# Windowed attention on one core: where ScalarE squares the queries, and where VectorE inverts the row sums

## The chip, the cores and the metric

One core of a Trainium2 chip runs the whole program in one launch. The metric is the device time in microseconds (us), as the median of several executions. PE is TensorE, ACT is ScalarE, DVE is VectorE, POOL is GpSimd.

## The reference

The input x is (4, 512, 256). A gated linear recurrence, a cross attention block with its own MLP, and then two layers of windowed attention with an MLP follow each other. Only the attention of the two layers is touched. Its core, for each of the two layers:

```python
q, k, v = jnp.split(shift_token(x) @ wqkv, 3, axis=-1)      # 8 heads of 64
q = l2norm(q) * qs;  k = l2norm(k) * ksc
q, k = rotary_xpos(q, k)                 # q*cos*scale + rotate_half(q)*sin*scale, k likewise
sim = einsum('bhwid,bhwjd->bhwij', q * 8, [previous window, own window] of k)
attn = softmax(where(mask, -max, sim));  out = einsum(attn, v)
x = x + out @ wo
```

The windows are 128 tokens. Each of the four sequences has four of them, so a layer has 16. The first window of a sequence has no predecessor and sees 128 keys, the others see 256.

## The kernel before, in words

The five engines run hand written instruction streams, joined by semaphores. Each wait is written out (`wait_ge(semaphore, count)`), and each engine executes its stream strictly in the order of the code. There is no planner.

The attention of a layer is a software pipeline over 16 windows n, with w the window's place in its sequence (0 to 3). In step n every engine's `window` function does the work on four tiles at once: scores, softmax and output of window n, transposition of the keys and queries of n+1 (`one`), projection of q, k and v, rotation and norms of n+2 (`two`), and the transposed input of n+3 (`three`). `two` holds in 14 of the 16 steps of a layer: the last two have nothing left to project. The eight heads are handled in four pairs i = 0 to 3; the pairs 0 and 1 use one couple of PSUM banks for scores, the pairs 2 and 3 another. A pair is two heads, so "the exponentials of a pair" are two instructions.

PE (`window`, L1944): scores of n (`score_pairs`, L1895); probabilities by values of n-1 (`weigh_values`, L1919); the projections of q and k of n+2 into banks 0 and 1 (`qkv` with i = 0 and 1, six matmuls each, recorded at L1593); transposition of the keys of n+1 (L1874); transposition of the probabilities of the pairs 0, 1, 2 (`transpose_probs`, L1905); transposition of the queries of n+1 (L1882), which waits for ACT's copy of the keys out of the same bank 2; the pair 3 of L1905; transposition of the spread reciprocal row sums (`transpose_sums`, L1929), which waits for POOL; the projection of v (L1593 again); the transposition of x of n+3 (L1851); the output projection of n-1 (L1941). `transpose_probs` waits until all four exponentials of its half (pairs 0 and 1, or 2 and 3) are done: the pairs 2 and 3 both wait for all eight.

ACT (`window`, L1482): `exps` for the pairs 0 to 3 (L1460, two instructions a pair, each with an accumulator read that gives the row sum), the square of the queries of n+2 (`square(n + 2, 0)`, L1431, which waits for their projection), the copy of the transposed keys of n+1 (`keys`, L1441), the square of the keys (L1431), the copies of the transposed probabilities (L1472), of the queries (L1447), of the sums (L1480), of v (L1436) and of x (L1423).

DVE (`window`, L1071): the masking with the row minimum for the eight heads (`masked`, L1048), `normalise` of n-1 (L1063), the norm scaling of the keys of n+1 (`norm_keys`, L1039), the reciprocal of the row sums (`invert_sums`, L1055, after all eight exponentials), the three rotation products of the queries of n+2 (`rope_products(..., 0)`, L1019 and twice L1024, after their square), those of the keys (`rope_products(..., 1)`), the sum of squares (L1031), the residual (L1069), the low part of x (L1101).

POOL: spreads the reciprocals over the head columns (L558), adds the rotation products of the queries and then of the keys (L551), computes the inverse norms (L567, L569), scales the queries (L573), splits MLP weights (L582, L584) and copies x (L543). It spreads before it rotates.

The waits that matter for the order:

```python
def square(n, i):   act.wait_ge(c_p, 3 * n + i + 1)      # projection i of tile n is done
def exps(n, w, i):  act.wait_ge(c_tt, 8 * n + 4 * (i // 2) + 4)
def transpose_probs(n, w, i): pe.wait_ge(c_ex, 8 * n + 4 * (i // 2) + 4)
def transpose_q(n, par):      pe.wait_ge(c_kt, n + 1)    # keys copied out of bank 2
def transpose_sums(n):        pe.wait_ge(c_rb, n + 1)    # POOL has spread the reciprocals
```

Of the kernel before, what the change touches and what calls it, by code (L numbers as in the profile page):

```python
# [27 lines left out]
TT = T // P  # L28
# [47 lines left out]
def build(nc, x, ctx_in, cols_in, rows_in, w_in, w_gate, w_out, wq, wk, wv, wo_x, pos_bias,  # L76
          w1_x, w2_x, lcols_in, qk_scale, rope, wqkv, wo_l, wm_l, out):
    with ExitStack() as ctx:
# [596 lines left out]
        def _(dve):  # L675
# [336 lines left out]
            def rope_products(n, w, i):  # L1012

                src = bank[i][:, :].rearrange("p (h d) -> p h d", d=DH)
                dve.wait_ge(c_sq, 2 * n + i + 1)
                if not (isinstance(n, int) and n == 0):
                    dve.wait_ge(c_add, 2 * n - 1 + i)
                cos = rope_l[:, 2 * i, w:w + 1, :].to_broadcast([P, HEADS, DH])
                dve.tensor_tensor(rot[:, 2 * i, :].rearrange("p (h d) -> p h d", d=DH), src, cos, ALU.mult)\  # L1019
                    .then_inc(c_rope, 1)  # L1020
                rotated = rot[:, 2 * i + 1, :].rearrange("p (h d) -> p h d", d=DH)
                for lo, other in ((0, DH // 2), (DH // 2, 0)):
                    sin = rope_l[:, 2 * i + 1, w:w + 1, lo:lo + DH // 2].to_broadcast([P, HEADS, DH // 2])
                    dve.tensor_tensor(rotated[:, :, lo:lo + DH // 2], src[:, :, other:other + DH // 2], sin,  # L1024
                                      ALU.mult).then_inc(c_rope, 1)

            def sum_squares(n):

                dve.wait_ge(c_sq, 2 * n + 2)
                dve.wait_ge(c_clip, n)  # L1030
                dve.tensor_reduce(norms[:, 0, :], squares[:, :, :].rearrange("p i (h d) -> p (i h) d", d=DH), AX_X,  # L1031
                                  ALU.add).then_inc(c_ss, 1)

            def norm_keys(n, par):

                dve.wait_ge(c_add, 2 * n + 2)
                dve.wait_ge(c_rn, n + 1)
                k = k_tok[:, par, :].rearrange("p (h d) -> p h d", d=DH)
                dve.tensor_tensor(k, k, norms[:, 2, HEADS:2 * HEADS].unsqueeze(2).to_broadcast([P, HEADS, DH]),  # L1039
                                  ALU.mult).then_inc(c_kn, 1)  # L1040

            def masked(n, w, i, first=False):

                nk = 2 * P if w else P
                wait_alone(dve, c_qk, 2 * n + i // 2 + 1)
                for e in range(2):
                    logits = bank[SCORES[i // 2] + e][:, (i % 2) * 2 * P:(i % 2) * 2 * P + nk]
                    dve.tensor_tensor_reduce(logits, logits, mask[:, 2 * P - nk:2 * P], 1.0, FAR, ALU.add, ALU.min,  # L1048
                                             row_min[:, w % 2, 2 * i + e:2 * i + e + 1]).then_inc(c_tt, 1)

            def invert_sums(n, w):

                dve.wait_ge(c_ex, 8 * n + 8)
                dve.wait_ge(c_rb, n)
                dve.reciprocal(row_rsum[:, :], row_sum[:, w % 2, :]).then_inc(c_ri, 1)  # L1055

            def normalise(n):

                dve.wait_ge(c_rt_out, n + 1)
                dve.wait_ge(c_pv, n + 1)  # L1060
                if not (isinstance(n, int) and n == 0):
                    dve.wait_ge(c_wo, n)
                dve.tensor_tensor(o_t[:, :, :].rearrange("p c t -> p (c t)"), bank[3][:, :], rsum_t[:, :], ALU.mult)\  # L1063
                    .then_inc(c_ot_out, 1)

            def att_residual(n, tile):

                dve.wait_ge(c_wo, n + 1)
                dve.tensor_tensor(inner[:, tile, :], inner[:, tile, :], bank[2][:, 0:D], ALU.add).then_inc(c_res, 1)  # L1069

            def window(n, t, w, l, prev, one, two, three):  # L1071
                for i in range(KI):
                    masked(n, w, i)
                if prev:
                    normalise(n - 1)
                if one:
                    norm_keys(n + 1, (w + 1) % 2)
                invert_sums(n, w)
                if two:
                    rope_products(n + 2, (w + 2) % TT, 0)  # L1080
                    rope_products(n + 2, (w + 2) % TT, 1)
                    sum_squares(n + 2)
                elif w == 2:
                    mlp_aggr(l * NB)
                if prev:
                    att_residual(n - 1, t - 1)
                if three:
                    x_low(n + 3, (w + 3) % TT, bank[1][:, 0:D])
                elif w == 1:
                    for i in range(TT):  # L1090
                        mlp_stats(l * NB, 0, i, 0)
                elif w == 2:
                    mlp_norm(l * NB, 0, 0)
                else:
                    input_low(l * NB)

            def x_low(n, w, src):

                dve.wait_ge(c_xt_out, n + 1)
                columns = slice(w * P, (w + 1) * P)  # L1100
                dve.tensor_tensor(x_lo[:, :].rearrange("p (c t) -> p c t", t=T + 1)[:, :, columns],  # L1101
                                  src.rearrange("p (c t) -> p c t", t=P),
                                  x_hi[:, :].bitcast(F32).rearrange("p (c t) -> p c t", t=T + 1)[:, :, columns],
                                  ALU.subtract).then_inc(c_xt_lo, 1)

            def mlp_stats(m, b, t, par):

                dve.wait_ge(landed[par], 32 * (m // 2) + 32)
                for i, src in enumerate((inner[:, b * TT + t, 0:P], shifts[par][:, t, :])):
                    dve.bn_stats(stats[:, t, 6 * i:6 * i + 6], src).then_inc(d_stats, 1)  # L1110

            def mlp_aggr(m):
                for t in range(TT):
                    wait_alone(dve, d_stats, 8 * m + 2 * t + 2)
                    dve.bn_aggr(mean_var[:, t, :], stats[:, t, :]).then_inc(d_aggr, 1)

            def mlp_norm(m, b, par):

                dve.wait_ge(d_rstd, m + 1)
                dve.wait_ge(d_tp, 2 * m)  # L1120
                for t in range(TT):
                    for i, src in enumerate((inner[:, b * TT + t, 0:P], shifts[par][:, t, :])):
                        dve.tensor_scalar(normed[:, t, i * P:(i + 1) * P], src, mean_var[:, t, 0:1],
                                          rstd[:, t:t + 1], ALU.subtract, ALU.mult).then_inc(d_norm, 1)

            def input_low(m):

                for c in range(KD):
                    dve.wait_ge(d_in_hi, 2 * m + c + 1)
                    dve.tensor_tensor(t_lo[:, c, :], h_t[:, c, :], t_hi[:, c, :].bitcast(F32), ALU.subtract)\  # L1130
                        .then_inc(d_in_lo, 1)
# [122 lines left out]
        def _(act):  # L1254
# [99 lines left out]
            def exps(b):  # L1354

                for m in range(KD):
                    act.wait_ge(b_kbias, 2 * b + m + 1)
                    act.activation(ek[:, m, :], bank[2 + m][:, :], ACT.Exp, bias=kstat[:, m, 2:3]).then_inc(b_ek, 1)
                    if m:
                        exp_q(b, 0)  # L1360
# [66 lines left out]
            def square(n, i):  # L1427

                act.wait_ge(c_p, 3 * n + i + 1)
                act.wait_ge(c_ss, n)  # L1430
                act.activation(squares[:, i, :], bank[i][:, :], ACT.Square).then_inc(c_sq, 1)  # L1431
# [50 lines left out]
            def window(n, w, l, prev, one, two, three):  # L1482
                exps(n, w, 0)
                exps(n, w, 1)
                exps(n, w, 2)
                exps(n, w, 3)
                if two:
                    square(n + 2, 0)
                if one:
                    keys(n + 1, (w + 1) % TT)  # L1490
                if two:
                    square(n + 2, 1)
                if not one:
                    mlp_scaled(l * NB, l)
                for i in range(KI - 1):
                    probs_transposed(n, w, i)
                if one:
                    queries(n + 1)
                probs_transposed(n, w, KI - 1)
                sums_transposed(n)  # L1500
                if two:
                    values(n + 2, (w + 2) % TT)
                if three:
                    x_transposed(n + 3, (w + 3) % TT, bank[1][:, 0:D])
                if not one:
                    mlp_rounded(l * NB)
# [665 lines left out]
```

## Time and profile before

| what | value |
|---|---|
| median of 3 executions | 992.8 us (991.03, 992.8, 993.05) |
| span of the profiled execution, first to last instruction | 990.8 us |
| PE busy | 924.9 us, 93% of the span |
| DVE busy | 675.9 us, 68% |
| ACT busy | 513.9 us, 52% |
| POOL busy | 422.6 us, 43% |
| granted TensorE clock, mean | 0.981 |

No separate time of the profiled execution is listed, only its span; the median lies 2.0 us above that span and the fastest execution 0.2 us above it. The attention steps of the first layer run from about 367 to 573 us of the span, those of the second from about 686 to 887 us. A step is read from the start of its first score matmul (L1895) to the next step's. The timeline gives for each engine the start, the duration, the line and the count of instructions merged, and in brackets the idle time ahead and what ended it.

### The profile page before, as it was taken

To read this page: it belongs to the slowest core of one execution; us is meant where nothing else is said; L and a number is where in the kernel's file an instruction comes from. 1 tells how busy PE (TensorE), PEld (TensorE's weight loads), DVE (VectorE), ACT (ScalarE), POOL (GpSimd) and SP (SyncE) were. 2 spreads that over 40 slices of the span, in tenths; PEclk is the share of its full clock that TensorE was granted. 3 is DMA by queue.
4 is the path that set the end of the run, shared out by engine and by line. 5 is a ranking of instruction groups with operands and counts; after the bars stand their busy time and mean duration, and the time that the engine had idled before them with its cause. 6 is when DMAs were issued, how large, how long until landed. Compare 5 with 4: busy or idle time off the path is not lost.

```text
span 990.8 us, 17519 instructions
## 1 busy us (share of the span) xinstructions
PE 924.9 (93%) x5688; PEld 774.2 (78%) x5688; DVE 675.9 (68%) x1706; ACT 513.9 (52%) x1221; POOL 422.6 (43%) x420
## 2 busy tenths in 40 slices
PE   5889996999999988999999899999999999889998
PEld 4668875787878866888888678887888888778887
DVE  6878797558687677677767555567766667735563
ACT  5467751313131426767666644454766666654443
POOL 5333354112221357767676400006776767631110
PEclk9889998999999999999999999999999999999999
DMA  7200123000000000000001030000000000000001
GB/s 261 70 1 16 48 65 112 1 1 0 0 0 1 1 23 1 2 23 0 22 0 33 12 105 15 4 25 2 2 24 0 22 0 12 27 15 17 31 25 46
DMA packets 15716, 26.34 MB, mean 27 GB/s; under 512 B 1642, under 2 KB 12256, under 8 KB 14896
## 3 DMA queue, kind: packets, MB, share of 16 engines
q1 hardware_dynamic: 15664, 25.69, 8.0%
q8 instruction: 27, 0.44, 0.2%
q14 instruction: 25, 0.20, 0.1%
HBM read 20.53 MB, written 2.10 MB: 23 GB/s over the span
## 4 chain that ended last, share of the span: by engine, by line
PE 72%; DVE 11%; ACT 6%; issue 3%; POOL 3%; SPq 3%; DMA 2%; ACTq 0%; DVEq 0%; POOLq 0%
PE bank L1593 33%; PE bank L1941 5%; PE bank L1895 5%; PE bank L1919 5%; PE bank L1801 5%; PE bank L1905 4%; ACT probs L1460 3%; PE bank L1764 2%; PE bank L1882 2%; PE bank L1747 1%; SPq L352 1%; DVE y L820 1%; PE bank L1929 1%; PE bank L2014 1%; PE bank L2011 1%
## 5 line engine op out<-in xcount | busy, mean ns | idle before, releaser
L1460 ACT ACTIVATE probs<-bank,row_min 128x256 f32<-128x256 f32 (+1 forms) x256 | 110.4, 458 | 120.1 <-DVE row_min L1048 120.1
L569 POOL TENSOR_TENSOR norms<-norms,minus_half 128x16 f32<-128x16 f32 x32 | 93.6, 2924 | 2.7
L1048 DVE CUSTOM_DVE_ANT_0 bank<-bank,mask 128x256 f32<-128x256 f32 (+1 forms) x256 | 90.7, 425 | 5.9 <-PE bank L1895 5.7
L1593 PE MATMUL bank<-wqkv_hi,x_hi 128*128 128x512 f32 x192 | 82.4, 429 | 1.8 <-DVE rot L1024 1.1
L1593 PE MATMUL bank<-wqkv_lo,x_hi 128*128 128x512 f32 x192 | 76.3, 397 | 0.0
L1593 PE MATMUL bank<-wqkv_hi,x_lo 128*128 128x512 f32 x192 | 75.7, 394 | 0.0
L1185 DVE SCALAR_TENSOR_TENSOR hidden<-bank,lcols,hidden 128x512 f32<-128x512 f32 (+1 forms) x48 | 36.0, 749 | 51.9 <-PE bank L1593 28.2
L551 POOL TENSOR_TENSOR q_tok<-rot 128x512 f32<-128x512 f32 x32 | 41.2, 1288 | 57.7 <-DVE rot L1024 57.7
L1905 PE MATMUL bank<-ident,probs 128*128 128x128 f32 x448 | 61.5, 279 | 3.9 <-ACT probs L1460 3.9
L1593 PE MATMUL bank<-t_hi,wm_hi 128*128 128x512 f32 x160 | 63.6, 397 | 0.0
L1593 PE MATMUL bank<-t_lo,wm_hi 128*128 128x512 f32 x160 | 63.5, 397 | 0.0
L1941 PE MATMUL bank<-wo_sb,o_t 128*128 128x256 f32 x256 | 60.9, 381 | 2.0 <-DVE o_t L1063 1.7
L1593 PE MATMUL bank<-t_hi,wm_lo 128*128 128x512 f32 x160 | 62.7, 392 | 0.0
L1069 DVE TENSOR_TENSOR inner<-inner,bank 128x256 f32 (+1 forms) x32 | 13.5, 421 | 71.9 <-PE bank L1941 71.9
L1895 PE MATMUL bank<-k_t,q_t 64*128 64x256 f32 (+1 forms) x512 | 57.9, 367 | 0.8 <-ACT q_t L1447 0.8
L1801 PE MATMUL bank<-w,ff 128*128 128x256 f32 x256 | 56.7, 379 | 0.0
L1905 PEld LDWEIGHTS bank<-ident,probs 128*128 128x128 f32 x448 | 52.5, 144 | 4.9 <-ACT probs L1460 4.9
L1019 DVE TENSOR_TENSOR rot<-bank,rope_l 128x512 f32<-128x512 f32 x64 | 43.9, 686 | 17.7 <-ACT squares L1431 17.7
L1460 ACT ACTIVATION_READ_ACCUMULATOR probs<-bank,row_min 128x1 f32 x256 | 55.5, 217 | 0.0
L1895 PEld LDWEIGHTS bank<-k_t,q_t 64*128 64x128 f32 x512 | 43.5, 190 | 14.0 <-issue 10.8
L1801 PEld LDWEIGHTS bank<-w,ff 128*128 128x128 f32 x256 | 48.5, 190 | 6.6
L1941 PEld LDWEIGHTS bank<-wo_sb,o_t 128*128 128x128 f32 x256 | 46.3, 190 | 8.0 <-DVE o_t L1063 2.2
(253 smaller groups left out, 2639.5 us busy)
## 6 DMA issues: line engine op xcount, KB each, us to landing
w_stage<-in_wm_l_dram SPq DMA_DIRECT2D x8, 534.0 KB, 3.7
w_stage<-in_wqkv_dram SPq DMA_DIRECT2D x2, 1536.0 KB, 8.0
out_dram<-stream SPq DMA_DIRECT2D x8, 256.0 KB, 2.4
emb<-in_ctx_dram SPq DMA_DIRECT2D x1, 1536.0 KB, 6.8
inner<-in_w_gate_dram SPq DMA_DIRECT2D x1, 1152.0 KB, 10.3
stream<-in_x_dram SPq DMA_DIRECT2D x2, 512.0 KB, 5.7
stream<-in_x_dram SPq DMA_DIRECT2D x1, 1024.0 KB, 12.8
ew<-in_pos_bias_dram SPq DMA_DIRECT2D x1, 1024.0 KB, 11.5
```

The costliest lines, as they stand in the source:

```text
L551: pool.tensor_tensor(dst[:, par, :], rot[:, 2 * i, :], rot[:, 2 * i + 1, :], ALU.add)\
L569: pool.tensor_tensor(norms[:, 2, :], norms[:, 1, :], minus_half[:, :], ALU.pow).then_inc(c_rn, 1)
L1019: dve.tensor_tensor(rot[:, 2 * i, :].rearrange("p (h d) -> p h d", d=DH), src, cos, ALU.mult)\
L1048: dve.tensor_tensor_reduce(logits, logits, mask[:, 2 * P - nk:2 * P], 1.0, FAR, ALU.add, ALU.min, row_min[:, w % 2, 2 * i + e:2 * i + e + ...
L1185: dve.scalar_tensor_tensor(hidden[0:r, i % 2, :], up[0:r, :], lcols[0:r, l, L_B1A + j:L_B1A + j + 1], hidden[0:r, i % 2, :], ALU.add, ALU. ...
L1460: act.activation(probs[:, i, e, 0:nk], logits, ACT.Exp, bias=row_min[:, w % 2, h:h + 1], scale=-1.0, accum_out=row_sum[:, w % 2, h:h + 1]) ...
L1593: ins = pe.matmul(out, stationary, moving, start=(first and i == 0), stop=(last and i == len(terms) - 1))
L1801: ins = pe.matmul(bank[6 + t // 2][:, (t % 2) * D:(t % 2 + 1) * D], ff[:, k, t * P:(t + 1) * P], w_2[:, k, :], start=(k == 0), stop=(k == ...
L1895: ins = pe.matmul(bank[SCORES[i // 2] + e][:, (i % 2) * 2 * P:(i % 2) * 2 * P + nk], q_t[half, i, :], k_t[half, i, k0:(w + 1) * P], start= ...
L1905: ins = pe.transpose(bank[SCORES[i // 2] + i % 2][:, (2 * e + k) * P:(2 * e + k + 1) * P], probs[:, i, e, k * P:(k + 1) * P], ident[:, :])
L1919: ins = pe.matmul(bank[3][e * DH:(e + 1) * DH, i * P:(i + 1) * P], v_tok[:, w - nk + 1 + k, h * DH:(h + 1) * DH], probs_ts[i][:, 2 * e + k ...
L1941: ins = pe.matmul(bank[2][:, 0:D], o_t[:, k, :], wo_sb[:, k, :], start=(k == 0), stop=(k == KI - 1))
```

## The change

On ACT the square of the queries of n+2 moves from behind the exponentials of the pairs 2 and 3 to between those of the pairs 1 and 2. On DVE the three rotation products of the queries of n+2 move ahead of the reciprocal of the row sums of n. No instruction is added or taken away, no wait's count changes, and PE's and POOL's streams stay as they are.

```diff
@@ DVE, window
                 if one:
                     norm_keys(n + 1, (w + 1) % 2)
+                if two:
+                    rope_products(n + 2, (w + 2) % TT, 0)
                 invert_sums(n, w)
                 if two:
-                    rope_products(n + 2, (w + 2) % TT, 0)
                     rope_products(n + 2, (w + 2) % TT, 1)
                     sum_squares(n + 2)
@@ ACT, window
                 exps(n, w, 0)
                 exps(n, w, 1)
+                if two:
+                    square(n + 2, 0)
                 exps(n, w, 2)
                 exps(n, w, 3)
-                if two:
-                    square(n + 2, 0)
                 if one:
                     keys(n + 1, (w + 1) % TT)
```

## Rows read from the trace of the kernel before

**Rows 1.** The page: busy time, share of the span and instructions of each engine.

```profile
PE 924.9 (93%) x5688; PEld 774.2 (78%) x5688; DVE 675.9 (68%) x1706; ACT 513.9 (52%) x1221; POOL 422.6 (43%) x420
```

**Rows 2.** Waits, 373 to 547 us: us in total, times, longest.

```profile
PEld bank L1882 <- ACT k_t L1441: 1.7, 6, 0.3
```

**Rows 3.** Timeline of ACT, a step with w = 2 (445.98 to 459.21 us).

```profile
449.03 0.47 ACT L1460 ACTIVATE probs<-bank,row_min 128x256 f32<-128x256 f32 x1 [3.73 <-DVE row_min L1048]
...
452.18 0.51 ACT L1460 ACTIVATE probs<-bank,row_min 128x256 f32<-128x256 f32 x1
452.54 0.24 ACT L1460 ACTIVATION_READ_ACCUMULATOR probs<-bank,row_min 128x1 f32 x1
452.63 0.64 ACT L1431 ACTIVATE squares<-bank 128x512 f32<-128x512 f32 x1
453.34 0.60 ACT L1441 ACTIVATE k_t<-bank 128x512 f32<-128x512 f32 x1
...
457.37 0.60 ACT L1436 ACTIVATE v_tok<-bank 128x512 f32<-128x512 f32 x1
457.87 0.38 ACT L1423 ACTIVATE x_hi<-bank 128x256 fp32r<-128x256 f32 x1
```

**Rows 4.** Timeline of PE, the same step.

```profile
451.07 0.39 PE L1593 MATMUL bank<-wqkv_hi,x_lo 128*128 128x512 f32 x1
...
453.14 1.47 PE L1905 MATMUL bank<-ident,probs 128*128 128x128 f32 x12
454.45 0.60 PE L1882 MATMUL bank<-ident,q_tok 128*128 128x128 f32 x4
...
455.32 0.60 PE L1929 MATMUL bank<-ident,rsum_heads 128*128 128x128 f32 x4
...
456.94 0.40 PE L1593 MATMUL bank<-wqkv_hi,x_lo 128*128 128x512 f32 x1
```

**Rows 5.** Timeline of ACT, a step with w = 1 (433.37 to 445.98 us).

```profile
436.41 0.47 ACT L1460 ACTIVATE probs<-bank,row_min 128x256 f32<-128x256 f32 x1 [4.01 <-DVE row_min L1048]
...
440.49 0.65 ACT L1441 ACTIVATE k_t<-bank 128x512 f32<-128x512 f32 x1
```

**Rows 6.** Timeline of PE, the step of rows 5.

```profile
437.58 0.39 PE L1593 MATMUL bank<-wqkv_hi,x_lo 128*128 128x512 f32 x1
...
441.19 0.66 PE L1882 MATMUL bank<-ident,q_tok 128*128 128x128 f32 x4
```

**Rows 7.** Timeline of ACT, a step with w = 0 (421.59 to 433.37 us).

```profile
423.69 0.37 ACT L1460 ACTIVATE probs<-bank,row_min 128x128 f32<-128x128 f32 x1 [3.07 <-DVE row_min L1048]
...
426.44 0.64 ACT L1431 ACTIVATE squares<-bank 128x512 f32<-128x512 f32 x1
428.11 0.60 ACT L1441 ACTIVATE k_t<-bank 128x512 f32<-128x512 f32 x1 [1.03 <-PE bank L1874]
```

**Rows 8.** Timeline of PE, the step of rows 7.

```profile
425.85 0.39 PE L1593 MATMUL bank<-wqkv_hi,x_lo 128*128 128x512 f32 x1
...
428.76 0.66 PE L1882 MATMUL bank<-ident,q_tok 128*128 128x128 f32 x4
```

**Rows 9.** Timeline of DVE, the step of rows 3.

```profile
452.81 0.20 DVE L1055 RECIPROCAL row_rsum<-row_sum 128x8 f32<-128x8 f32 x1 [1.21 <-ACT probs L1460]
453.39 0.69 DVE L1019 TENSOR_TENSOR rot<-bank,rope_l 128x512 f32<-128x512 f32 x1 [0.37 <-ACT squares L1431]
...
454.66 0.68 DVE L1019 TENSOR_TENSOR rot<-bank,rope_l 128x512 f32<-128x512 f32 x1
```

**Rows 10.** Timeline of POOL, the step of rows 3.

```profile
453.14 0.61 POOL L558 COPY rsum_heads<-row_rsum 128x512 f32<-128x512 f32 x1 [1.27 <-issue]
```

**Rows 11.** Timeline of PE, the step before last of layer 1, then of layer 2.

```profile
554.10 1.47 PE L1905 MATMUL bank<-ident,probs 128*128 128x128 f32 x12
...
865.88 1.09 PE L1874 MATMUL bank<-ident,k_tok 128*128 128x128 f32 x4 [2.54 <-DVE k_tok L1039]
866.76 2.64 PE L1905 MATMUL bank<-ident,probs 128*128 128x128 f32 x12
```

## The prediction

> **What bounds the kernel now.** I read the page first: PE is busy 93% of the span, no other engine over 68% [rows 1]. Shares mix stages, so I then took the timelines of the attention steps, the only stage touched. They repeat in three forms. With w = 2 or 3 a step takes 13.2 us, with w = 1 12.6 us, with w = 0 11.8 us. In the steps with w = 2 and 3 PE never waits. In those with w = 1 and w = 0 it waits once, before it transposes the queries, for ACT's copy of the keys out of the shared bank: 1.7 us in six waits in layer 1 [rows 2], a little under 0.3 us each. So a step is PE's own work and, in two forms of four, a short stop behind ACT. Only what moves a PE start can change the time.
>
> The reader should see where ACT stands against PE. For w = 2, ACT begins the eight exponentials at 449.03 and ends the last accumulator read at 452.54 + 0.24 = 452.78 [rows 3]; PE begins the transposition of the probabilities at 453.14, the queries at 454.45, the sums at 455.32 [rows 4].
>
> **The change, part by part.** *The square between the exponentials.* Eight starts lie between 449.03 and 452.18 in seven steps: 0.45 us each [rows 3]. Four exponentials free ACT at 449.03 + 4 x 0.45 = 450.83. There the square now waits for the projection of the queries, whose sixth matmul starts at 451.07 [rows 4]. What is queued behind it on ACT is the second half of the exponentials, and PE's transpositions behind those. When is a projection released? The one of v shows it: sixth matmul at 456.94 [rows 4], copy at 457.37 [rows 3], 0.43 us later. So the square starts at 451.50, after 0.67 us idle. An instruction of this size that follows an idle time occupies 457.87 - 457.37 = 0.50 us [rows 3], so the exponentials resume at 452.00 and free ACT at 453.80. The last accumulator read ends 452.78 - 452.18 = 0.60 us behind the last start, at 453.35 + 0.60 = 453.95, against 452.78 before. The keys' copy starts at 453.80 instead of 453.34: before, it was held back by PE anyway (the square began at 452.63 and the step to the copy was 0.71, not 0.48).
>
> Now PE. The 12 transpositions from 453.14 on take (454.45 - 453.14) / 12 = 0.11 us each [rows 4]; the first eight wait for the first half of the exponentials, which is not later than before. The ninth was due at 454.02, and its weights some 0.1 us ahead; it is released at 453.95. So it loses between 0 and 0.1 us. The queries need the copy of the keys: 453.80 + 0.60 to 0.65 (both durations occur [rows 3, 5]) = 454.40 to 454.45, and PE starts 0.05 us behind it, as from 440.49 + 0.65 = 441.14 to 441.19 with w = 1 [rows 5, 6]. That is 454.45 to 454.50 against 454.45 before, and a transposition that has waited hides its first weight load less: 0.66 against 0.60 for the four [rows 4, 6]. I take 0.10 us, by these nearest rows; the ends are 0 and 0.25. Twelve steps have this form with `two` (w = 2 and 3, three sequences, two layers): 12 x 0.10 = **1.2 us**. It cannot be below nothing: PE has no wait here that could shrink.
>
> With w = 1 the first four exponentials free ACT at 436.41 + 4 x 0.45 = 438.21, and the projection is released at 437.58 + 0.43 = 438.01 [rows 5, 6]. No wait: square and exponentials only change places, and the copy stays at 440.49. The pairs 2 and 3 end 0.5 us later, inside the stop that PE makes for this copy. Eight steps at **0**, ends 0 and 0.1 us; the cover is that stop of under 0.3 us.
>
> With w = 0 the exponentials see 128 keys and step by (426.44 - 423.69) / 8, that is 0.34 us [rows 7]; the square is released at 425.85 + 0.43 = 426.28 [rows 8], then 0.50 and 4 x 0.34 give 428.14 for the copy against 428.11 [rows 7]. Its 0.60 may become 0.65, since the idle time ahead of it goes. PE's queries at 428.76 [rows 8] move by 0.03 to 0.08 us. I take 0.07: six steps, **0.4 us**, ends 0 and 0.6. The two first steps of a layer have their chain in front of the copy too, and no wait for the projection: 0.
>
> *The rotation products ahead of the reciprocal.* Three instructions of DVE, 454.66 - 453.39 = 1.27 us together [rows 9], go ahead of the reciprocal. With w = 2 they start once the square ends, 451.50 + 0.60 and some 0.1 us, and end at 453.5, before the exponentials are through. The reciprocal then starts at 453.98 instead of 452.81 [rows 9]. POOL's spread follows it by 453.14 - 452.81 = 0.33 and takes 0.61 [rows 9, 10]: done at 454.92, and PE wants it at 455.32 less a weight load of 0.1 [rows 4]. 0.3 us of cover, so nothing. With w = 0 the cover is thinnest, about 0.1 us by the same sum, and with w = 1 0.4 us. If it were gone, each step would pay the excess alone. POOL's rotation of the queries comes behind the spread now, at 454.92; before it came behind the products, which ended about 454.66 [rows 9] and some 0.2 us of handing over: the same time. For the keys DVE starts at 454.9 to 455.0 instead of 454.66 [rows 9], since their square follows the later copy; POOL's norms move 0.15 us, with over 1 us before the next step's key scaling asks for them. On SP nothing is moved; on POOL no instruction changes place.
>
> Sum against the profiled execution: 990.8 + 1.2 + 0.4 + 0 = 992.4 us of span. The median of the runs lies 2.0 us above that span, so against the median: 992.8 + 1.6 = **994.4 us**. The 1.6 us are 0.16%. About 0.2%, 2.0 us, is the least that a measurement of this kernel can tell from no change, its own three runs spreading over 2.0 us.
>
> *A rule that speaks against the change.* Exponential and square now alternate one time more per step. The square already follows the last exponential with a step of 0.45 us, from 452.18 to 452.63 [rows 3], the same as between exponentials. The Trainium skill (ScalarE: Activation LUTs, "Table sets: the hidden batching unit") says to batch activations by set, and gives about 2.7 us for each switch to another set; were square in another set, 28 steps with two more switches would cost some 150 us, an estimate from that page. The trace shows no switch in that direction.
>
> **The rivals.** *Nothing on PE's path.* If the ninth transposition and the queries' both just fit, the cost is 0: 992.8 us. For it: each estimate misses PE's old start by 0.05 us or less. Against: two such fits in all 12 steps.
>
> *ACT's delay reaches PE in full (slower).* The place is the second half of the exponentials with w = 2 and 3, held by the square behind the projection. It decides once the release comes later than 0.43 us after the sixth matmul, or the step after the idle time is longer than 0.50: PE's cover is used up, and all further delay is paid 12 times. The copy is 453.80 - 453.34 = 0.46 us later. Paid whole, that is 12 x 0.46 = 5.5 us: 998.3 us; with half of it 995.6. For it: zero slack on both PE starts. Against: the release has a row of its own.
>
> *POOL and the next step gain (faster).* With w = 1 the square comes at 438.21 instead of 0.48 us ahead of the copy at 440.49 [rows 5], so the products of the queries end near 440.2 (before, they could not begin ahead of 440.6), and those of the keys follow some 0.5 us earlier; POOL's norms and the key scaling of the next tile could too. Were that chain what ends last, eight steps would give 0.5 us each: 988.8 us. Against: DVE does not wait for POOL there, it works through eight masks first.
>
> *The exponential behind a square pays a reload.* The direction from square to exponential stands nowhere close together; the first exponential of a step has up to 4.01 us of idle time in front [rows 5] in which it could hide. As a mechanism of this kernel it costs at most 28 x 4.0 = 112 us, 1,105 us. This is the rule of the Trainium skill cited above (ScalarE: Activation LUTs).
>
> One thing moves all cases: in the step before last, PE stops for 2.54 us, and in layer 2 its clock falls behind that: 12 transpositions take 2.64 us, where the same step of layer 1 shows 1.47 [rows 11]. A shift in time can add or take one such fall, 1.2 us.
>
> **How the numbers follow.** My sum 0.55, no cost 0.17, full delay 0.16, POOL's gain 0.11, reload 0.01. The sum's own ends are 0 and 3.6 (12 x 0.25 + 0.6) us, so 992.8 to 996.4, widened by the clock below, and above into the half-way case of the delay: 991.0 to 997.6 us leaves out the gain, the reload and the worst third of the full delay. Of my sum's 0.55 I give 0.37 to within 0.2% and 0.18 to slower; with the others: same 0.54, slower 0.35, faster 0.11.
>
> **What would show it.** Right: with w = 2 ACT idles about 0.67 us ahead of the square for PE L1593; the keys' copy comes 0.46 us later; waits of PE's weight loads L1882 for k_t or L1905 for probs appear in 12 more steps, under 0.15 us each; the step stays at 13.2 to 13.4 us. With w = 1, 12.6 us again, and the reciprocal some 0.45 us later. Wrong: steps of 13.5 us or more, a wait of L1929 for POOL, steps below 13.2, or an idle time between square and exponential.

## The result, and the profile after

Over 19 executions each, the changed kernel takes 994.29 us (988.58 to 996.79) and the kernel before 990.56 us (987.89 to 993.35). The ratio is 1.004, 95% interval 1.0027 to 1.0053: slower by 3.7 us, clear of the 0.2% bound. The forecast of 994.4 us lies next to the measured time by luck. Three executions had given 992.8 us for the kernel before, and 19 give 990.56, so the base was 2.2 us too high; the step forecast was 1.6 us and the step measured is 3.7, so the step was 2.1 us too small. One execution of e1, at 3,228 us, is slow and left out of all that follows.

The profiled execution of the changed kernel has a span of 994.2 us, 3.4 more than the one before, and a mean granted clock of 0.976 against 0.981. Its page, busy times, to be set beside [rows 1]:

```profile
PE 930.7 (94%) x5688; PEld 778.3 (78%) x5688; DVE 678.2 (68%) x1706; ACT 513.3 (52%) x1221; POOL 419.8 (42%) x420
```

The count of instructions is the same and PE is 5.8 us longer busy. That is the first hint that something beside waiting happened: instructions got longer.

**The steady steps.** The timeline of ACT, a step with w = 2 (446.22 to 459.48 us), answers to [rows 3]:

```profile
449.27 0.47 ACT L1461 ACTIVATE probs<-bank,row_min 128x256 f32<-128x256 f32 x1 [3.72 <-DVE row_min L1048]
...
451.72 0.60 ACT L1432 ACTIVATE squares<-bank 128x512 f32<-128x512 f32 x1 [0.52 <-PE bank L1594]
452.22 0.47 ACT L1461 ACTIVATE probs<-bank,row_min 128x256 f32<-128x256 f32 x1
...
454.02 0.62 ACT L1442 ACTIVATE k_t<-bank 128x512 f32<-128x512 f32 x1
```

The square waits for the projection and holds the second half of the exponentials; the copy of the keys starts 7.80 us into the step, where it was 7.36. PE in the same step, against [rows 4]:

```profile
453.36 1.50 PE L1906 MATMUL bank<-ident,probs 128*128 128x128 f32 x12
454.70 0.65 PE L1883 MATMUL bank<-ident,q_tok 128*128 128x128 f32 x4
455.18 0.60 PE L1906 MATMUL bank<-ident,probs 128*128 128x128 f32 x4
455.62 0.60 PE L1930 MATMUL bank<-ident,rsum_heads 128*128 128x128 f32 x4
```

From the twelve transpositions to the queries it is 1.34 us (before 1.31), from there to the last pair 0.48 (0.43): two stretches of 0.03 and 0.05 us, too short to be listed as waits. What the waits view of 373 to 547 us does list, against [rows 2], is three waits for the keys, those with w = 0, and three new ones for the third pair's exponentials, in the steps with w = 1, where PE waited for the keys before:

```profile
PEld bank L1883 <- ACT k_t L1442: 0.9, 3, 0.3
PEld bank L1906 <- ACT probs L1461: 0.8, 3, 0.3
```

DVE and POOL, against [rows 9] and [rows 10]:

```profile
452.44 0.69 DVE L1019 TENSOR_TENSOR rot<-bank,rope_l 128x512 f32<-128x512 f32 x1 [0.62 <-ACT squares L1432]
453.05 0.75 DVE L1024 TENSOR_TENSOR rot<-bank,rope_l 128x256 f32<-128x256 f32 x2
454.18 0.20 DVE L1055 RECIPROCAL row_rsum<-row_sum 128x8 f32<-128x8 f32 x1 [0.38 <-ACT probs L1461]
```

```profile
454.50 0.62 POOL L558 COPY rsum_heads<-row_rsum 128x512 f32<-128x512 f32 x1 [3.31 <-issue]
```

The spread ends at 455.12, half a microsecond ahead of PE's sums at 455.62. So the cover held.

To add the steps up, I take the starts of the score matmuls. PE's timeline of the changed kernel, steps 0, 13, 14 and 15 of layer 1, then of layer 2:

```profile
367.17 1.79 PE L1896 MATMUL bank<-k_t,q_t 64*128 64x128 f32 x16
535.47 2.00 PE L1896 MATMUL bank<-k_t,q_t 64*128 64x256 f32 x16
547.68 2.00 PE L1896 MATMUL bank<-k_t,q_t 64*128 64x256 f32 x16
560.70 2.00 PE L1896 MATMUL bank<-k_t,q_t 64*128 64x256 f32 x16
687.81 1.16 PE L1896 MATMUL bank<-k_t,q_t 64*128 64x128 f32 x16 [0.67 <-ACT q_t L1448]
849.84 2.00 PE L1896 MATMUL bank<-k_t,q_t 64*128 64x256 f32 x16
862.06 2.00 PE L1896 MATMUL bank<-k_t,q_t 64*128 64x256 f32 x16
875.07 2.00 PE L1896 MATMUL bank<-k_t,q_t 64*128 64x256 f32 x16
```

The same instructions of the kernel before:

```profile
367.08 1.86 PE L1895 MATMUL bank<-k_t,q_t 64*128 64x128 f32 x16
535.00 2.00 PE L1895 MATMUL bank<-k_t,q_t 64*128 64x256 f32 x16
547.20 2.00 PE L1895 MATMUL bank<-k_t,q_t 64*128 64x256 f32 x16
559.07 2.00 PE L1895 MATMUL bank<-k_t,q_t 64*128 64x256 f32 x16
685.67 1.16 PE L1895 MATMUL bank<-k_t,q_t 64*128 64x128 f32 x16 [0.83 <-ACT q_t L1447]
847.24 2.00 PE L1895 MATMUL bank<-k_t,q_t 64*128 64x256 f32 x16
859.44 2.00 PE L1895 MATMUL bank<-k_t,q_t 64*128 64x256 f32 x16
872.56 2.00 PE L1895 MATMUL bank<-k_t,q_t 64*128 64x256 f32 x16
```

| stretch | before | after | more |
|---|---|---|---|
| up to step 0 of layer 1 | 367.08 | 367.17 | 0.09 |
| steps 0 to 12, layer 1 and 2 | 167.92, 161.57 | 168.30, 162.03 | 0.84 |
| step 13, both | 12.20, 12.20 | 12.21, 12.22 | 0.03 |
| step 14, layer 1 | 11.87 | 13.02 | 1.15 |
| step 14, layer 2 | 13.12 | 13.01 | -0.11 |
| step 15 and the MLP, layer 1 | 126.60 | 127.11 | 0.51 |
| step 15 and the rest, layer 2 | 118.24 | 119.13 | 0.89 |

The sum is 3.40 us, and 0.84 + 0.03 of it is where the change is; 0.09 lies ahead of it. The other 2.44 us are in the steps 14 and 15 and behind, where neither `square` nor `rope_products` runs at all.

**The last steps.** PE of the changed kernel in layer 1, steps 14 and 15, to be set beside [rows 11]:

```profile
554.12 0.63 PE L1875 MATMUL bank<-ident,k_tok 128*128 128x128 f32 x4 [2.54 <-DVE k_tok L1039]
554.59 2.12 PE L1906 MATMUL bank<-ident,probs 128*128 128x128 f32 x12
556.50 1.06 PE L1883 MATMUL bank<-ident,q_tok 128*128 128x128 f32 x4
...
566.85 1.09 PE L1906 MATMUL bank<-ident,probs 128*128 128x128 f32 x8 [1.24 <-ACT probs L1461]
568.68 1.79 PE L1906 MATMUL bank<-ident,probs 128*128 128x128 f32 x8 [0.74 <-ACT probs L1461]
```

The stop ahead of them is 2.54 us, as before, yet four transpositions of the queries now take 1.06 us, where the same form takes 0.60 to 0.65 at the full clock. The windows view gives the granted clock of these stretches (PEclk, third column from the right):

```profile
555.00:560.00 5.00, 5.00 (x28) 4.87 (x27) 0.49 (x5) 3.96 (x9) 3.20 (x5) 0.66 0.07 20
568.00:573.00 5.00, 4.32 (x18) 4.03 (x19) 0.20 (x1) 5.00 (x13) 2.93 (x8) 0.66 0.01 2
869.00:873.00 4.00, 4.00 (x24) 4.00 (x22) 0.49 (x5) 3.25 (x8) 2.91 (x5) 0.57 0.09 24
882.00:887.00 5.00, 4.26 (x20) 3.86 (x19) 0.20 (x1) 5.00 (x13) 2.92 (x8) 0.66 0.00 1
```

Four stretches partly at 1.2 GHz, behind the stops of steps 14 and 15 in both layers. Such a stretch is called a fall of the clock below. The kernel before has the same stops and the full 2.4 GHz in three of these places:

```profile
552.00:557.00 5.00, 3.25 (x28) 3.04 (x28) 1.98 (x9) 5.00 (x18) 1.89 (x5) 1.00 0.07 20
565.00:570.00 5.00, 4.05 (x27) 3.54 (x28) 0.47 (x2) 5.00 (x16) 2.56 (x7) 1.00 0.01 2
866.00:869.00 3.00, 3.00 (x15) 3.00 (x16) 0.49 (x5) 2.34 (x7) 1.61 (x3) 0.50 0.09 25
879.00:884.00 5.00, 4.16 (x28) 3.24 (x26) 0.28 (x2) 5.00 (x15) 2.92 (x8) 1.00 0.00 0
```

This is no accident of one trace. Every execution lists its mean granted clock. Over 19 executions of the changed kernel it averages 0.9793; over 97 of the kernel before, run beside the experiments, 0.9844 (0.9841 to 0.9845 in each of their four groups). The times follow it:

| mean granted clock | before: executions, median us | after: executions, median us |
|---|---|---|
| 0.976 to 0.977 | none | 8, 996.1 |
| 0.979 to 0.982 | 23, 992.9 | 9, 993.0 |
| 0.983 to 0.984 | 39, 990.9 | none |
| 0.986 to 0.987 | 18, 988.7 | none |
| 0.988 to 0.991 | 17, 988.2 | 2, 988.8 |

The only listed value that both kernels reach is 0.988: one execution of the changed kernel, 989.07 us, against 988.16 us, the median of 17 of the kernel before. These 0.9 us are about what the steady steps give, but one execution proves little, and the clock is listed in steps of 0.001, over which the kernel before moves by about 0.7 us (0.981 to 0.988: 4.8 us). The larger part of the 3.7 us is that the changed kernel gets the low clocks more often.

### The profile page after: what moved, and what is told of

The parts are those of the page before. It is cut to its first block, busy times and chain, and to the rows that moved or that the text cites. A ratio compares the mean times of both kernels' runs of the same rounds, so it can differ in the third digit from the quotient of the medians.

```text
span 994.2 us, 17519 instructions
## 1 busy us (share of the span) xinstructions
PE 930.7 (94%) x5688; PEld 778.3 (78%) x5688; DVE 678.2 (68%) x1706; ACT 513.3 (52%) x1221; POOL 419.8 (42%) x420
## 4 chain that ended last, share of the span: by engine, by line
PE 74%; DVE 11%; ACT 5%; POOL 3%; issue 3%; DMA 1%; SPq 1%; ACTq 0%; DVEq 0%; POOLq 0%
PE bank L1594 34%; PE bank L1942 6%; PE bank L1896 5%; PE bank L1802 5%; PE bank L1920 5%; PE bank L1906 5%; ACT probs L1461 2%; PE bank L1883 2%; PE bank L1765 2%; PE bank L1930 2%; PE bank L1748 1%; DVE y L820 1%; DVE normed L1124 1%; PE bank L2015 1%; PE bank L2012 1%
## 5 line engine op out<-in xcount | busy, mean ns | idle before, releaser
L1906 PE MATMUL bank<-ident,probs 128*128 128x128 f32 x448 | 66.3, 289 | 4.6 <-ACT probs L1461 4.2
L558 POOL COPY rsum_heads<-row_rsum 128x512 f32<-128x512 f32 x32 | 19.7, 616 | 108.6 <-DVE row_rsum L1055 59.2
L1432 ACT ACTIVATE squares<-bank 128x512 f32<-128x512 f32 x64 | 39.5, 616 | 26.8 <-PE bank L1594 26.8
```

The costliest lines, as they stand in the source:

```text
L1906: ins = pe.transpose(bank[SCORES[i // 2] + i % 2][:, (2 * e + k) * P:(2 * e + k + 1) * P], probs[:, i, e, k * P:(k + 1) * P], ident[:, :])
```

## The experiments

Theory A: ACT's second half of the exponentials, held behind the projection, reaches PE by a fraction of its delay, 0.84 us in all. Theory C: the rest is the clock, which falls behind the stops of the last steps more often because these stops come at another time. The rivals are B, that the later reciprocal costs, and plain chance.

### e1: the square alone

Against the changed kernel:

```diff
@@ DVE, window
-                if two:
-                    rope_products(n + 2, (w + 2) % TT, 0)
                 invert_sums(n, w)
                 if two:
+                    rope_products(n + 2, (w + 2) % TT, 0)
                     rope_products(n + 2, (w + 2) % TT, 1)
```

> Only the square moves between the exponentials; the products stay behind the reciprocal. Measure: the time from the first score matmul of step 0 to that of step 13 of a layer (before 167.92 and 161.57 us, with the whole change 168.30 and 162.03 us), free of the last steps. Theory A (ScalarE's second half of the exponentials, held behind the projection, reaches TensorE): all of the 0.38 and 0.46 us is there, steps with w = 2 and 3 are 13.26 us. Rival B (the later reciprocal makes TensorE wait for the sums): the two stretches are back at 167.9 and 161.6 us. Clock theory C (most of the 3.7 us is additional falls of TensorE's clock behind the stops of the last two steps): the time is spread like that with the whole change, around 993 to 994 us, and what exceeds 0.9 us goes with the mean granted clock.

Measured: 992.63 us, 1.0017 times before (1.0003 to 1.0032). The two stretches are 168.44 and 162.17 us, the steps with w = 2 and 3 take 13.262 us on average (before 13.217, changed kernel 13.262). So the stall is the square's alone, and B falls. The steps with w = 0 take 11.85 us, 0.05 more than with the whole change: the products' place gives a little back there (6 x 0.05 = 0.3 us). Theory C's figure is missed: the time lies below 993 to 994 us, at a mean clock of 0.9824, between the changed kernel (0.9793) and the kernel before (0.9844), although both stretches are as long as in the changed kernel. Their length alone does not set how often the clock falls.

### e2: the products alone

Against the changed kernel:

```diff
@@ ACT, window
                 exps(n, w, 1)
-                if two:
-                    square(n + 2, 0)
                 exps(n, w, 2)
                 exps(n, w, 3)
+                if two:
+                    square(n + 2, 0)
```

> Only the products of the queries go ahead of the reciprocal; the square stays behind all exponentials. The reciprocal now comes behind the square and 1.3 us of products. Theory A: with w = 2 the reciprocal starts 1.7 us later (about 8.6 us into the step), the spread ends at 9.5, and TensorE's sums, due at 9.34, wait 0.2 to 0.3 us in the steps with w = 2, 3 and more with w = 1 (due 8.75, ready 9.5: 0.8 us): the stretch of step 0 to 13 grows by 7 to 10 us over two layers. Rival B (the sums have the cover that I gave them in all forms): no growth. It is the half of the change that needs the other half.

Measured: 1002.55 us, 1.0137 (1.0112 to 1.0162). The steps with w = 1 take 13.67 instead of 12.70 us, those with w = 2 and 3 13.60 instead of 13.22. The waits view of 373 to 547 us names it (line, who for, us in total, times, longest):

```profile
PEld bank L1930 <- POOL rsum_heads L558: 6.3, 10, 1.0
PE bank L1930 <- POOL rsum_heads L558: 4.0, 10, 0.8
```

The growth over both stretches is 13.0 us, more than the 7 to 10 expected: with w = 1 the stop is a full microsecond. The mechanism is the one expected. The reciprocal may stand behind the products only if the square has come early. The products need the early square; the square does not need the products (e1).

### e3: the change, with the square one pair later

```diff
@@ ACT, window, against the changed kernel
                 exps(n, w, 1)
-                if two:
-                    square(n + 2, 0)
                 exps(n, w, 2)
+                if two:
+                    square(n + 2, 0)
                 exps(n, w, 3)
```

> The change, with the square behind the exponentials of pair 2 instead of pair 1. With w = 2 and 3 ScalarE comes to it at 5.75 us of the step, when the projection is released (5.50): no idle time, last exponential and keys' copy as before. Theory A: both stretches are back at 167.9 and 161.6 us within 0.1. Rival B (what costs is the square anywhere between exponentials, or the later reciprocal): they stay at 168.3 and 162.0 us. Clock theory C: total time like before, 990.6 us, if the shift of 0.4 us a layer is what brings the clock falls; if not, it stays above 992.

Measured: 989.09 us, 0.9997 of before (0.9979 to 1.0014), mean clock 0.9863. The steps with w = 2 and 3 are back at 13.209 us, those with w = 0 at 11.77. ACT has no idle time ahead of the square any more:

```profile
447.02 0.49 ACT L1461 ACTIVATE probs<-bank,row_min 128x256 f32<-128x256 f32 x1
447.38 0.23 ACT L1461 ACTIVATION_READ_ACCUMULATOR probs<-bank,row_min 128x1 f32 x1
447.47 0.62 ACT L1432 ACTIVATE squares<-bank 128x512 f32<-128x512 f32 x1
447.95 0.51 ACT L1461 ACTIVATE probs<-bank,row_min 128x256 f32<-128x256 f32 x1
```

So it is the wait for the projection that costs there, not a square between exponentials. The stretches as wholes are not back, though (168.14 and 162.15 us). Their sum is 0.80 us above the kernel before, as much as in the changed kernel (0.84): the stall has moved. The steps with w = 1 take 12.763 us (changed kernel 12.707), and the first step of layer 2 takes 9.06 us instead of 8.67, with PE's sums 0.34 us later in it. The trace of that step shows why:

```profile
687.47 0.19 DVE L1055 RECIPROCAL row_rsum<-row_sum 128x8 f32<-128x8 f32 x1
688.47 0.66 PE L1930 MATMUL bank<-ident,rsum_heads 128*128 128x128 f32 x4 [0.18 <-POOL rsum_heads L558]
```

It is the wait of e2 on a small scale: the square comes later, the products behind it, the reciprocal behind them, and the sums wait for POOL. With w = 1 no wait is listed, but the four sums take 0.66 us instead of 0.60, as after a wait. The square one pair later with the products left behind the reciprocal was not run. For theory C this run is no clean test: the stretches grew as much as in the changed kernel, and still the time and the clock are those of the kernel before, with no fall in either step 14 of the trace (11.89 and 11.88 us).

### e7: the square waits longer

```diff
@@ ACT, window, against the changed kernel
                 if two:
+                    act.wait_ge(c_p, 3 * (n + 2) + 2)
                     square(n + 2, 0)
```

> The change, and the square also waits for the projection of the keys, 1.40 us later. Theory A: the cover is used up, so with w = 2 and 3 all of it is paid, 12 x 1.4 = 17 us, with w = 1 (release 6.04 against 4.86) 1.2 less the stop of 0.2, 8 x 1.2 us, and with w = 0 (6.10 against 4.68) 6 x 1.4: 33 to 36 us in all, about 1,028 us. Rival B (ScalarE's delay is mostly hidden and something else costs): under 15 us.

Measured: 1030.7 us, 1.041 (1.0385 to 1.0436). Over both stretches 36.0 us more than in the changed kernel (186.10 and 180.24), at the upper end of theory A's figure. PE, a step with w = 2 of this kernel (451.40 to 466.20 us):

```profile
458.56 1.04 PE L1907 MATMUL bank<-ident,probs 128*128 128x128 f32 x8
460.93 0.66 PE L1907 MATMUL bank<-ident,probs 128*128 128x128 f32 x4 [1.34 <-ACT probs L1461]
461.42 0.65 PE L1884 MATMUL bank<-ident,q_tok 128*128 128x128 f32 x4
```

The place of the wait is the ninth transposition, as the forecast had it, and delay beyond the cover is paid about one for one: the square comes 7.05 us into the step instead of 5.50, and the steps with w = 2 and 3 take 14.80 us instead of 13.26. In the changed kernel the cover is just about exhausted.

### e4 and e5: filling TensorE's stop in step 14

```diff
@@ PE, window, against before (e4) and against the changed kernel (e5)
                     qkv(n + 2, (w + 2) % TT, 1)
+                elif one:
+                    pe.wait_ge(c_v, NT * (l + 1))
+                    pe.wait_ge(c_rope, 6 * NT * (l + 1))
+                    product(bank[1][:, :], [(x_hi[:, (i % 4) * P:(i % 4 + 1) * P],
+                                             wqkv_hi[:, 0, 0:INNER]) for i in range(5)] * 2)
```

> The kernel before, with ten more matmuls (2.35 us) in each layer's step before last, where TensorE stops for 2.54 us; they write a bank that nobody reads afterwards. Clock theory C: without the stop, the clock has less reason to fall; executions at the low granted clocks of the kernel before (0.981) become rare, the median drops by 1 to 2 us, to about 989 us, and the spread narrows. Rival (the falls behind the last steps come from elsewhere): no change of the median within 0.1%, or slower by what overshoots the stop.

> The changed kernel with the same ten matmuls in the same place. Clock theory C: the loss beyond the 0.9 us of stalls goes with the stop of the last steps; this kernel comes out about 1 to 2 us above the filled kernel before (990 to 991.5 us) instead of 3.7. Rival (the change costs 3.7 us in its steady steps, which one trace did not show): it stays 3 us or more above the filled kernel before.

Measured: the filled kernel before 989.85 us, 0.9992 (0.9975 to 1.0008); the filled changed kernel 989.80 us, 0.9997 (0.9981 to 1.0012). Both steps 14 take 11.89 us in both traces. The filling does little for the kernel before (clock 0.9853), less than expected, but takes the whole loss from the changed one, more than forecast: its clock rises from 0.9793 to 0.9868, and its trace has no fall in the steps 14 and 15. Its steady steps still carry their stall, 168.40 and 162.03 us. The rival, 3 us or more between the two, falls. In e4's trace the clock falls once in step 15 of layer 2, whose stops this filling leaves.

### e6 and e8: shifting the last steps

```diff
@@ PE, window, against before (e6, 2) and against the changed kernel (e8, 5)
                 if two:
+                    if not three:
+                        pe.wait_ge(c_rope, 6 * (n + 2) + 3)
+                        product(bank[0][:, :], [(x_hi[:, 0:P], wqkv_hi[:, 0, 0:INNER])] * 2)
                     qkv(n + 2, (w + 2) % TT, 2)
```

> The kernel before, with two more matmuls (0.47 us) ahead of the projection of v in step 13 of each layer: its last steps start as much later as those of the changed kernel, and nothing else differs. Clock theory C: it loses more than the 0.94 us it adds: falls behind step 14 in most executions, median 993 to 995 us. Rival (the falls are chance, the same for all kernels): 991.9 us, before plus 0.94.

> The changed kernel with five more matmuls (1.17 us) in the same place, 2.3 us of added work. Clock theory C with the place of the last steps deciding: the falls behind step 14 change in number, so the time is not the sum; it could be as low as 993 us. Rival (chance alone, or a cost in the steady steps): 994.3 + 2.3 = 996.6 us.

Measured: e6 993.24 us, 1.0029 (1.0012 to 1.0046), mean clock 0.9812. The kernel before, with 0.94 us of harmless matmuls in step 13, loses 2.9 us; the added work alone would be 1.0009, just outside the interval. Its one trace, of an execution of 988.31 us at a clock of 0.990, has no fall in the steps 14 and 15 (the windows view gives 1.00 from 541 to 560 us), so no trace shows where the clock of the slower executions falls. e8 takes 993.81 us, 1.0037 (1.0022 to 1.0052), mean clock 0.9840: 2.3 us of work are added to the changed kernel and it does not get slower. Its trace has a fall in step 14 of layer 1 (13.18 us) and none in that of layer 2 (11.89). Neither time fits a sum of costs well; both are what C allows, without showing its mechanism. In e8 step 13 takes 13.39 us instead of 12.21, so the work was done.

### e11: shifted and filled

The shift of e6, the ten matmuls of e4 in step 14, and twelve narrow ones in step 15:

```diff
@@ PE, window
+                if not one:
+                    product(bank[2][:, D:2 * D], [(x_hi[:, 0:P], wqkv_hi[:, 0, 0:D])] * 8)
                 for i in range(KI - 1):
+                    if not one and i == 2:
+                        product(bank[2][:, D:2 * D], [(x_hi[:, 0:P], wqkv_hi[:, 0, 0:D])] * 4)
                     transpose_probs(n, w, i)
```

> The kernel before, with the two matmuls that shift each layer's last steps by 0.47 us, and with the stops of the steps 14 and 15 filled. The shift alone cost 2.9 us for 0.94 us of work. Clock theory C: the excess of 2 us comes from the clock falling behind those stops, so with the stops filled the shift costs its 0.94 us only, and the filling gives some back: 989.5 to 991.5 us, and a granted clock of 0.984 or more on average. Rival (the place of the rest of the program in time decides, not these stops): 993 us again.

Measured: 991.22 us, 1.0005 (0.9986 to 1.0023), mean clock 0.9858. Against e6 2 us are gone although more matmuls run. The intervals of e6 and e11 overlap a little (1.0012 to 1.0023), so this alone would be weak. It points the same way as e5, which ties the loss to these stops.

### e9 and e10: more stops filled

The filling of e11 without its shift, on the kernel before (e9) and the changed one (e10), and nine matmuls ahead of `transpose_k` in step 0 of layer 1:

```diff
@@ PE, window
+                if not prev and l == 0:
+                    product(bank[3][:, :], [(x_hi[:, 0:P], wqkv_hi[:, 0, 0:INNER])] * 9)
```

> The kernel before, with matmuls into unread halves of banks in three stops of TensorE: nine in step 0 of layer 1 (stop 4.14 us), ten in step 14, twelve narrow ones in step 15 (stops 1.23 and 0.73 us). Clock theory C: the falls at about 377 us and behind steps 14 and 15 go, each of which costs about 1.1 us; the median is 987 to 988.5 us, faster than before by 0.2 to 0.3%, and the spread narrows. Rival (the falls come whatever TensorE does there): 990 us as before.

> The changed kernel with the same matmuls. Clock theory C: with the stops filled, what is left of the change's cost is the 0.9 us of its steady steps: 988 to 989.5 us. Rival (chance, or a cost of the change elsewhere): 3 us or more above the other kernel of this pair.

Measured: e9 989.19 us, 0.9989 (0.9974 to 1.0003); e10 990.64 us, 1.0009 (0.9994 to 1.0023). Half a miss: both come out 1 us above the forecast, and e9 is not clearly faster than before. In both profiles the clock still falls in step 0 at about 375 us. The nine matmuls take 2.21 us of the 4.14, and a stop is left:

```profile
374.81 0.66 PE L1874 MATMUL bank<-ident,k_tok 128*128 128x128 f32 x4 [2.13 <-DVE k_tok L1039]
```

Whether a stop filled to its end would keep the clock up there was not run. The difference of the pair is 1.45 us, that of the pair e4 and e5 -0.05. Each ratio is known to about 0.15%, 1.5 us, so the pairs cannot test the 0.84 of the steady steps; neither shows 3.7.

## Why the prediction was right, and where it was not

*The wait on the projection.* Right in place and close in size. The square came at 5.50 us of the step (forecast 451.50 - 445.98 = 5.52), 0.65 us after ACT's slot for it (forecast 0.67; the view's 0.52 counts from the end of the last accumulator read), the keys' copy at 7.80 (7.82). The twelve steps lost 12 x 0.045 = 0.54 us, where I took 12 x 0.10 = 1.2. The twelve more waits that I named as a sign are not listed, each is too short. e7 shows that the cover ends where I put it, and e3 that the wait is the cause in these steps.

*Steps with w = 1.* Right: 12.707 against 12.695 us on average. PE's stop did not grow, it moved from the queries to the third pair. The reciprocal came 0.50 us later into the step (forecast 0.45).

*Steps with w = 0.* 6 x 0.04 = 0.24 us against 0.4 forecast. That the products' new place gives some back (e1) I had not seen.

*The reciprocal.* Right with w = 2: start 7.96 us into the step, forecast 8.00, and no wait of the sums for POOL anywhere in the stretch. e2 shows the price when that cover is missing, 13 us.

*The sum and the clock.* Here the prediction failed, although the time fell inside its range. The whole forecast, 1.6 us, was made of stalls; these measured 0.84, half of it. The term that was mis-sized most is the clock: "A shift in time can add or take one such fall, 1.2 us." I named the right place, step 14, but treated it as a symmetric uncertainty worth one fall. In the profiled execution it was three falls more, 2.4 us, and over all executions the mean granted clock went from 0.9844 to 0.9793. I should have asked how often each of the four stops of the last steps brings a fall in the kernel before; one in four in its trace meant that there was more to lose than to gain. So the slower outcome had 0.35 where it deserved more than the 0.54 of no change.

*The rivals.* The full delay of 5.5 us fell (PE's cover took all but 0.045 of 0.44 us in each step). POOL's gain fell: its rotation of the queries came 0.68 us earlier into the step with w = 1 (8.24 against 8.92) and nobody waited for it. The reload did not show: an exponential follows the square after 0.50 us with w = 2, and after 0.48 us without an idle time in e3. The trace shows no switch between square and exponential in either direction. The Trainium skill's rule on batching by table set (ScalarE: Activation LUTs, "Table sets: the hidden batching unit") therefore has nothing to say against this order.

*What stays open.* The runs show that most of the loss is clock, and that it goes when the stop of step 14 is filled (e5). They do not show why the change brings more falls. Why the same stop of 2.54 us is followed by a fall in one execution and not in another was not settled either. That its place in time decides is supported by e6, whose interval just excludes the plain sum, and by e8, but two runs do not fit a simple form of it: e1 has stretches as long as the changed kernel's and half of its loss, and e3 has about the same growth and no loss. What "place" would mean is open too, as step 0 of layer 1 starts anywhere from 360.91 to 368.17 us of the span in the traces of these kernels, far more than the shifts of 0.4 us. The Trainium skill (TensorE: Matmul & The Clock Gate, Part 1) also says that the number of slow matmuls changes from run to run with the phase of the gate. The spread of the clocks over executions of one kernel, 0.981 to 0.988 before, agrees with it, but no run here shows the phase.

No experiment gave a version clearly faster than both. The nearest by its ratio is e9, 0.9989, 1.6 us below before with an interval that includes no change.

## What to carry to other kernels

Moving an instruction that waits to the front of a queue delays all that is behind it: find the time at which its input is released, and put it just behind as much ready work as fills that gap. e3 does so and loses its stall with w = 2 and 3, but then look at what waits for the moved instruction in turn: there the reciprocal did, and a stall of the same size came up in other steps. Where the pace setting engine has stops elsewhere, cost a change also by what its shift does to TensorE's clock behind them, and compare executions at an equal granted clock before blaming or crediting an edit: a difference of 0.4% can lie in steps that the change never touches.

## What the runs showed that was not expected

Adding 0.94 us of matmuls to the kernel before cost 2.9 us (e6); adding 2.3 us to the changed kernel cost nothing (e8); ten matmuls into a bank nobody reads made the changed kernel 4.5 us faster (e5, 994.29 to 989.80). And nine matmuls in a stop of 4.14 us, which left 2.13 us of it, did not keep the clock from falling right behind it (e9), at 375 us as before.
